# A one-layer perceiver kernel: where the second expert is rounded, when the squares are summed, and where the first down projection stands

## The reference

```
x = x + cross_attention(layernorm(x), context)      # 16 heads
x = x + mixer(layernorm(x))                          # selective scan, 1024 channels, 16 states
x = x + ffn(layernorm(x)), where ffn is
    x1 = x + silu(pointwise(depthwise_conv3(x)))
    moe = out_w @ (sum over the top 2 of 8 experts of share * silu(expert_w @ x1)) + out_b
    h = norm_w * (x1 + moe) / rms(x1 + moe)
    ffn = h + ff_up(gelu(ff_down(h)))
```

## Time and profile before

| | |
|---|---|
| median of 3 runs | 2072.3 us (2068.81 to 2079.34) |
| the profiled execution: its own time | 2070.83 us |
| its span, first to last instruction | 2069.0 us |
| mean granted clock of PE | 0.981 of 2.4 GHz |
| busy share of the span | PE 95%, DVE 69%, POOL 58%, ACT 45% |
| experts' stage | from 1744.8 us to the end |

### The profile page before, as it was taken

How to read it: one execution, slowest core, us unless ns; L and a number is a source line. 1 busy time by engine, 2 the same in 40 slices (tenths; PEclk the granted TensorE clock), 3 DMA queues, 4 the chain that set the end, 5 groups by cost and what they waited for, 6 DMA issues and landing times. The chain is left out here.

```text
span 2069.0 us, 41932 instructions
## 1 busy us (share of the span) xinstructions
PE 1959.9 (95%) x15620; PEld 1429.0 (69%) x15620; DVE 1425.7 (69%) x1479; ACT 929.4 (45%) x1332; POOL 1208.4 (58%) x862
## 2 busy tenths in 40 slices
PE   6989999999999999999997879989999999999998
PEld 5867777777777777777774458655655554658886
DVE  4126767666666666666766754399999998538675
ACT  4124444444444444444433544376676664533340
POOL 4126666666666666666666631079998996325210
PEclk9999999999999999999997889999999999999999
DMA  5545555555555554555544320040040002111201
GB/s 187 162 131 174 156 182 161 175 168 164 173 164 172 162 175 153 176 157 182 169 131 135 109 80 1 17 109 1 1 122 1 1 1 98 41 42 61 92 11 41
DMA packets 180570, 229.58 MB, mean 111 GB/s; under 512 B 21488, under 2 KB 111920, under 8 KB 174224
## 3 DMA queue, kind: packets, MB, share of 16 engines
q1 hardware_dynamic: 180368, 226.82, 35.3%
HBM read 153.18 MB, written 73.56 MB: 110 GB/s over the span
## 5 line engine op out<-in xcount | busy, mean ns | idle before, releaser
L504 POOL TENSOR_TENSOR a_half<-a_pt 128x1024 f32<-128x1024 f32 x128 | 306.8, 2397 | 346.2 <-ACT a_pt L571 336.2
L571 ACT ACTIVATE a_pt<-a_shift 128x2048 f32<-128x2048 f32 x128 | 245.2, 1915 | 474.6 <-PE a_o L887 370.9
L685 DVE TENSOR_TENSOR a_shift<-a_s,a_neg_rows 128x2048 f32<-128x2048 f32 x113 | 259.0, 2292 | 170.8 <-ACT a_neg_rows L588 170.8
L672 DVE TENSOR_REDUCE a_top<-a_s 128x128 f32<-128x2048 f32 x113 | 258.8, 2290 | 46.1 <-PE a_s L840 46.1
L1274 POOL TENSOR_TENSOR s_even_drive<-s_du,l_rows 128x512 f32<-128x512 f32 x128 | 162.8, 1272 | 62.4 <-DMA s_c_row<-bc_scratch 60.0
L799 PE MATMUL a_pj<-l_x_hi,l_w_hi 128*128 128x512 f32 x448 | 199.1, 445 | 0.0
L495 POOL TENSOR_TENSOR l_x_lo<-a_raw,l_x_hi 128x512 fp32r<-128x512 f32 x120 | 152.9, 1274 | 72.5 <-ACT l_x_hi L558 72.5
L799 PE MATMUL a_pj<-l_w_hi,l_x_hi 128*128 128x512 f32 x448 | 185.6, 414 | 0.0
L1282 POOL TENSOR_TENSOR s_odd_seen<-s_odd_state,s_c_row 128x512 f32<-128x512 f32 x128 | 162.4, 1269 | 34.7 <-DVE s_odd_state L1413 16.1
L1474 PEld LDWEIGHTS s_ps<-s_diag,s_du_t 128*128 128x128 f32 x1024 | 135.9, 194 | 61.9 <-issue 61.9
L801 PE MATMUL a_pj<-l_x_lo,l_w_hi 128*128 128x512 f32 x448 | 177.8, 397 | 0.1
(11 more groups left out here) (270 smaller groups left out, 4077.5 us busy)
## 6 DMA issues: line engine op xcount, KB each, us to landing
kv_scratch<-a_k_new SPq DMA_DIRECT2D x128, 256.0 KB, 2.5
kv_scratch<-a_v_new SPq DMA_DIRECT2D x128, 256.0 KB, 3.5
a_stack<-kv_scratch SPq DMA_DIRECT2D x512, 64.0 KB, 2.3
a_v<-kv_scratch SPq DMA_DIRECT2D x32, 1024.0 KB, 5.9
a_raw<-in_ctx SPq DMA_DIRECT2D x120, 256.0 KB, 3.3
a_q_stack<-q_scratch SPq DMA_DIRECT2D x128, 64.0 KB, 1.9
s_c_row<-bc_scratch SPq DMA_DIRECT2D x32, 256.0 KB, 6.1
e_ew_raw<-in_ew SPq DMA_DIRECT2D x8, 1024.0 KB, 4.8
```

Of the source, the lines that this page charges most:

```text
L504: nc.gpsimd.tensor_tensor(half[:], w[:, 0:2], w[:, 2:4], ALU.add).then_inc(halved, 1)
L571: nc.scalar.activation(pt_head(g, p), shift[:].rearrange("p (i n) -> p i n", n=BANK), ACT.Exp).then_inc(exped, 1)
L672: dve.tensor_reduce(top[:], s_ps[:].rearrange("p i n -> p (i n)").rearrange("p (k q) -> p q k", q=L), AX.X, ALU.max).then_inc(blocked, 1)
L685: dve.tensor_tensor(shift[:].rearrange("p (k q) -> p k q", q=L), s_ps[:].rearrange("p i n -> p (i n)").rearrange("p (k q) -> p k q", q=L), ...
```

## The change

Three edits, all in experts:

1. POOL takes the rests of expert 1 behind the rest of the last batch, and ACT rounds expert 1 at b == 6 in place of b == 4. Expert 0 stays.
2. The squares are summed tile by tile: behind output(n) PE sums tile n - 1 (four matmuls, one for each batch of the group), and tile 7 is summed behind down(0). The first matmul of a group carries the start flag, the last one the stop flag. On DVE root_of_squares(0) follows tile 4, and scale_group(0) tile 5, with tiles 6 and 7 behind them. spread(0) on PE follows output(5).
3. down(0) stands right behind the last tile of output (and tile 6's squares), and turn_back(3) is moved ahead of the up projections.

```diff
             for b in range(2, B):
                 rest_of_output(b)
-                if 3 <= b < 3 + 4:
-                    rest_of_expert((b - 3) // 2, (b - 3) % 2)
+                if b in (3, 4):
+                    rest_of_expert(0, b - 3)
+            for half in range(2):
+                rest_of_expert(1, half)
...
-                if b == 1 or b == 4:
-                    round_expert(b // 4)
+                if b == 1 or b == 6:
+                    round_expert(b // 6)
...
-            for n in range(NT - 1):
+            for n in range(KC + 1):
                 add_output(n)
             root_of_squares(0)
-            add_output(NT - 1)
+            add_output(KC + 1)
             scale_group(0)
+            for n in range(KC + 2, NT):
+                add_output(n)
             root_of_squares(1)
...
-            def squares(g, bs):
-                pe.wait_ge(hp_out, square_no(KC * g + KC - 1))
-                for b in bs:
-                    for k in range(KC):
-                        mm = pe.matmul(ps[:, 4 + g, b:b + 1], h_t[:, k, batch(BG * g + b)], ones[:, 0:1], start=(k == 0),
-                                       stop=(k == KC - 1))
-                if bs[-1] == BG - 1:
+            def squares(n):
+                k, g = n % KC, n // KC
+                pe.wait_ge(hp_out, square_no(n))
+                for b in range(BG):
+                    mm = pe.matmul(ps[:, 4 + g, b:b + 1], h_t[:, k, batch(BG * g + b)], ones[:, 0:1],
+                                   start=(k == 0 and b == 0), stop=(k == KC - 1 and b == BG - 1))
+                if k == KC - 1:
                     mm.then_inc(ss_made, 1)
...
             for n in range(NT):
                 output(n)
-                if n >= KC and n < NT - 1:
-                    squares(0, ((0,), (1,), (2, 3))[n - KC])
-            spread(0)
-            squares(1, range(BG))
+                if n >= 1:
+                    squares(n - 1)
+                if n == KC + 1:
+                    spread(0)
             down(0)
+            squares(NT - 1)
             turn_back(0)
             turn_back(1)
             spread(1)
             turn_back(2)
+            turn_back(3)
             up(0)
             up(1)
             up(2)
-            turn_back(3)
             down(1)
             up(3)
```

## The result

The changed kernel takes 2060.88 us (median of 13 runs, 2055.85 to 2068.22) against 2070.23 us for the kernel before (13 runs, 2065.5 to 2079.34). The ratio is 0.9956, 95% interval 0.9945 to 0.9968: 9.1 us less, between 6.6 and 11.4. The forecast was 2061.5 us, its sum 10.0 us less. In the profiled executions the spans are 2059.8 and 2069.0 us.

The account below looks back on a forecast made before the run. PE (95% busy) bounds the kernel, with two waits worsened by slow clock; 6.5 + 3.5 = 10.0 us off 2070.8 gives 2060.8, median 2062.3, middle 2061.5 us; range 2057.5 to 2067.5, main case 2059 to 2064.

Parts of the forecast that it names:

- Edit 1, 6.5 us: At batch 6, ending PE's wait for POOL saves 6.5 us, stall and slow clock together; lower bound 4.9.
- The tightest place: At pointwise(0), which needs tile 3's taps: 0.45 us to spare after the change, against 1.8 before.
- The rounding on ACT: Expert 1's rounding, 1.91 us behind normalise(6), ends at 1795.9; nothing queues behind it before batch 7's root.
- The meeting of POOL's second half with the taps of tiles 4 to 7: Ahead of pointwise(4), POOL's half delays DVE's taps about 1.1 us, at most 2.4; cost zero, with 1.6 of cover.
- The tail, 3.5 us: From the output projection to down(1), edits 2 and 3 save 3.5 us; bounds 4.7 and 0.
- The walk through the list: PE's new tail timed item by item from output(0) at 2011.24: down(1) starts at 2050.56 against 2054.10 before.
- The new wait of 0.7: Before spread(1), PE waits 0.7 us for its diagonal, until 2046.24.
- It split the tail's gain: Tail: 2.2 squares' records, 1.6 down(0), 0.9 PE's wait, less four interruptions at 0.15 and the new 0.7: 3.4 us.
- after either wait PE runs at 0.50: After the waits for POOL and DVE's squares, PE runs at 1.2 GHz, so each costs more than its length.
- The clock didn't fall in the new tail: Rival, chance 0.2: half clock for 3 to 7 us in the tail costs 1.5 to 3.5 us; 2063 to 2065.
- the slower side: Rival, chance 0.04: squares between output tiles pull down the clock, costing up to 30 us more; 2091.
- The taps were not late: Rival, chance 0.1: late taps at pointwise(0) or pointwise(4) cost at most 2.5 us; 2062 to 2064.

Follow-up runs that it names:

- fill_stall: Kernel before plus five extra float32 matmuls of 512 columns ahead of batch 6, where PE waits for POOL; ratio 0.9987 (0.9974 to 1.0).
- pool_side_only: Kernel before with only POOL's two halves of expert 1 moved, ACT still rounding at b == 4; ratio 0.9993 (0.9984 to 1.0002).
- fill_wait: Kernel before plus one extra 512-column matmul between spread(0) and the last squares, where PE waits for DVE; ratio 0.9978 (0.9964 to 0.9992).
- squares_first: Changed kernel without edit 3: tile 7's squares ahead of down(0), turn_back(3) behind the ups; ratios to before 0.9955 and, repeated, 0.9944.

## Why the prediction was right

**Edit 1, 6.5 us.** Measured 6.51 on A, and 6.55 alone. The way of getting it, from the spacing of three turns, took stall and clock together without having to know either; fill_stall splits them into 4.8 and 1.7.

**What is late next.** Nothing. The tightest place was named rightly: 0.45 us to spare at pointwise(0) by the sum, 0.36 in the trace. The rounding on ACT ends at 1796.5, the root for batch 7 starts at 1796.81, so it queues nothing. The meeting of POOL's second half with the taps of tiles 4 to 7, given at 1.1 us, cost 0.3: eight taps took 6.21 in place of 5.89, the first of them 1.08, from 1800.73 to 1801.81, with POOL at work until 1801.26. By the Trainium skill, "SBUF — State Buffer", section "Who interferes with whom", the tap waits until POOL's instruction is over. The trace agrees: the tap ends 0.55 us behind POOL's instruction, just as tile 0's two taps did before (1785.20 behind 1784.64, 1787.94 behind 1787.39). pool_side_only shows such a meeting where nothing covers it.

**The tail, 3.5 us.** Measured 3.33. The walk through the list foresaw the start of the second down projection 39.32 us behind the first output matmul (2050.56 - 2011.24) and it came at 39.53. The difference is tile 0's squares (0.90 in place of 0.81; DVE had written them at 2010.72, 0.07 us ahead of the first of these matmuls, and the trace names no wait) and the first down projection (3.52 in place of 3.43). The new wait of 0.7 came as forecast: spread(1) starts 1.57 us behind two turns that take 0.88, and 0.50 of the 0.69 between them shows as idle time.

**What the prediction had wrong on the way.** It split the tail's gain into 2.2 for the squares' records, 1.6 for the down projection and 0.9 for the wait, less 1.3. Priced at full clock the 32 records take 3.59, not 4 x 0.81 = 3.24, so only 1.8 of the first term was slow clock. The new list interrupts three output tiles more than the old one (six against three), as the prediction's own walk has it, not four. And turn_back(3) already stood ahead of down(1) in the old list, so that nothing changes behind it. None of this touches the walk, from which the 3.5 came. A reading of the mechanism was wrong: "after either wait PE runs at 0.50" holds for the stall, where fill_stall took the idle time away and the slow clock went with it. Behind the wait for the squares the clock stayed at 1.00 for another 1.6 us, and in fill_wait it fell without that wait.

At full clock the old list would have B = 42.86 - 3.3 = 39.6, the new one's; this is worked out, for no profile shows the old tail without a slow stretch. By it all of the tail's gain is clock: the 0.87 us of the wait removed and the 0.3 saved on the squares are paid back by the new 0.7 and the three interruptions.

**The rivals.** The clock didn't fall in the new tail in any of its three profiles, and the squares between output tiles left it at 1.00, so that the slower side had nothing to stand on. The taps were not late. That the gain of the tail would depend on how long the old one ran slow, between 1.7 and 5.0 us, was not among the rivals: I took one profile's loss, 3.3, as the kernel's. That this profile lay in the middle of the six (1.7, 1.7, 3.3, 3.3, 3.4, 5.0) and gave 3.5 against 3.33 was luck. So is part of how near the time came: the forecast started from a median of 2072.3 us for the kernel before, which more runs brought down to 2070.23, and missed the gain by 0.9 us but the time by 0.6. The gain, 0.44%, lies just under the 0.5% that the prediction took for its border, with 0.48 on either side.

## What to carry to other kernels

Where an in-order engine feeds the bound one, look at which of its instructions waits for something that nobody needs yet: here POOL stood for 8.11 us before a half of an expert that was wanted over 70 us later (expert 0 comes first, and its products start at 1836.01 in the trace of before), and the next batch's input was rounded 4.7 us before POOL got to move. Move both sides of such a hand-over, since moving one alone only shifts the collision. Spread TensorE's thin matmuls between full ones: as a block of 32 records they took 3.6 us here and lost 1.7 to 5.0 more by the clock behind them. And compare kernels by the length of the stage in their traces when the runs scatter by more than the gain.

## What the runs showed of the hardware that I had not expected

- Behind 3.59 us of one-column matmuls without any idle time the granted clock fell from 1.00 to 0.50 (fill_wait, one profile). The Trainium skill, "TensorE: Matmul & The Clock Gate", section "What's actually happening", has the gate follow how busy PE has been recently. By the records alone the trace doesn't bear that out: they have PE busy without a gap from 2038.32 until the clock fell.
- The same list of instructions loses different amounts: 1.7, 3.3 and 5.0 us in the old tail, 0 and 1.7 in squares_first. A slow stretch in one profile is one draw.
- In the changed kernel 0.81 us of one-column matmuls, four turns, one full product and 0.50 us of idle time in a row (2038.09 to 2042.30) left the clock at 1.00.
